# Expert loop of a gated two-layer kernel: the second product of an expert moved one place back, butterfly stages multiplied in pairs, and the shared expert spread differently over the program

## Chip, cores and metric

The kernel runs on one core of one Trainium2 chip. The metric is the device time in microseconds (us) of one execution. The engines are PE (TensorE), DVE (VectorE), ACT (ScalarE), POOL (GpSimd) and SP (SyncE, which only issues DMAs here).

## What is computed

The input is x of 4 x 1024 tokens with 256 features. Four blocks are added to it in turn, each with a gate.

```python
x = x + tanh(g_xattn[0]) * L0_xattn(layernorm(x), ctx)   # 16 heads, stablemax, 154 keys
x = x + tanh(g_ffn[0])   * L0_ffn(layernorm(x))          # 64 experts, top 8, capacity 128, + shared expert
x = x + tanh(g_xattn[1]) * L1_xattn(layernorm(x), ctx)   # softmax attention
x = x + tanh(g_ffn[1])   * L1_ffn(layernorm(x))          # butterfly MLP
```

In the L0 feed-forward block each expert works on up to 128 gathered tokens: `silu(x @ Wg) * (x @ Wu) @ Wd`, 128 inner features, scattered back with the routing weight. A shared expert with 512 inner features works on all tokens.

The L1 feed-forward block is `butterfly(gelu(butterfly(x @ W_exp + b) + up_bias)) @ W_con`. A butterfly on 1024 features has ten stages. Stage s replaces feature i by `own[i] * y[i] + other[i] * y[i ^ 2**s]`. The butterflies don't depend on x, so the kernel folds them into W_exp and W_con beforehand: after that the block is two plain products.

## The kernel before, in words

The program has three stages, with all engines drained between them. Each is a plan, a list of named units written out by `plan_first`, `plan_experts` and `plan_last`; every engine runs its own part of each unit, in the order of the plan and in no other. So a unit that waits on an engine holds up all that stands behind it on that engine.

- `plan_first`: L0 attention, over 8 halves of 512 tokens, and the gate.
- `plan_experts`: at its start 14 tiles (`TAIL_TILES` 18 to 31) of `hots` and `place`, which count tokens into the lists of the experts: DVE makes two one-hot tiles, ACT scales one, and PE adds four matmuls (L935). One step of the shared expert stands behind each tile. Then come `lists` (with a round trip through memory), three more shared steps and `tokens`. Then comes the loop over 64 experts.
- `plan_last`: L1 attention and the butterfly MLP, pipelined over the 8 halves, 20 chunks each. Half 0 has its search for the largest scores (`peak`, L987/L989 on PE, L1694 on DVE) ahead of the pipeline.

The loop takes experts in overlapping places. In iteration n the PE runs `down(n-5)` (the second product, L967), `gate_up(n-4)` (the first product, L958), `turn(n-3)` (the transposes of the gathered rows, L948), and POOL runs the scatter (L1813) of `down`'s result and the gather (L1805) of expert n. Between `gate_up(e)` and `down(e)` stand ACT's silu (L1226) and DVE's product `inner` (L1657). `gate_up(e)` itself waits for `inner(e-1)`, since both use one bank; `down(e)` waits for DVE's `made(e-1)` (L1664).

Two streams fill the gaps of the loop. `back` holds the steps of the shared expert; in one half of 512 tokens they are four steps with `sh_up` (12 matmuls of 128x512, L882), one step with none, and two `sh_down` (24 matmuls of 128x256, L898). `fusing` holds the folding of the butterflies: for seven stages of each of the two butterflies and 8 blocks of 128 features, ACT scales the identity (`stage_p`, L1182), DVE adds the scaled swap (`stage_m`, L1589), PE multiplies (`inside`, L917) and ACT brings the result back (L1189). The three other stages are `across` (ACT and DVE alone). One fusing step stands behind `down` and one behind `turn`.

`LATE = 2` says that the shared expert's last two halves (6 and 7) stand in `plan_last`, one step behind two `peak` units each; `BEHIND = 4` steps stand behind the end of the loop.

## Time and profile before

| | |
|---|---|
| median of 3 runs | 1270.5 us (1266.7 to 1273.0) |
| profiled execution | 1270.4 us, span 1268.6 us |
| busy over the span | PE 84%, DVE 63%, PEld (PE's weight load) 61%, ACT 58%, POOL 28% |
| mean granted TensorE clock | 0.919 of full speed |
| matmuls and weight loads | 5713 each; DVE 1988 instructions, ACT 1447 |
| chain that ended last | PE 52%, DVE 21%, ACT 14% |

The busy shares are means over three stages with different limits, so they don't say what one edit is worth. Ends of matmuls are modelled; the distance from one start to the next is the better measure of what a group of matmuls costs. An f32 matmul is recorded as two instructions, a rounded one (fp32r) as one.

### The profile page before, as it was taken

What the parts mean: (1) busy time and instruction counts of PE and PEld (TensorE: products, weight loads), DVE (VectorE), ACT (ScalarE), POOL (GpSimd) and SP (SyncE); (2) the same over time, 40 slices, a digit from 0 to 9 for tenths busy, and PEclk for the clock granted to TensorE, in tenths of its full rate; (3) what the DMA queues carried; (4) which work ended last, traced back from release to release, by engine and by line L of the source; (5) the groups of instructions that cost most, each with busy time, mean ns of one, the idle gap of its engine ahead of it and who ended that gap; (6) DMA issues with size and microseconds to landing.
All of it is one profiled execution on the core that took longest, in us unless ns stands there. A gap on an engine that the chain in (4) does not pass through costs nothing.

```text
span 1268.6 us, 17757 instructions
## 1 busy us (share of the span) xinstructions
PE 1063.4 (84%) x5713; PEld 770.4 (61%) x5713; DVE 802.0 (63%) x1988; ACT 732.5 (58%) x1447; POOL 357.1 (28%) x313
## 2 busy tenths in 40 slices
PE   3788888888876788998899868778989989999988
PEld 2344444444444677876688756646766767767567
DVE  4568778777777654555654476566676676765443
ACT  1998888898964335665665432344455445544542
POOL 2000000000000004777777420204253342423223
PEclk9788888898877998999999979868999999999998
DMA  6554535442120305889887352230232132220000
GB/s 152 122 134 138 141 80 156 133 113 71 51 104 33 141 18 149 210 197 226 215 208 187 52 158 65 71 98 1 77 87 86 26 102 58 64 70 1 20 17 17
DMA packets 97404, 128.44 MB, mean 101 GB/s; under 512 B 26976, under 2 KB 69344, under 8 KB 97056
## 3 DMA queue, kind: packets, MB, share of 16 engines
q1 hardware_dynamic: 83312, 106.91, 29.3%
q0 software_dynamic: 12288, 18.88, 8.2%
q10 hardware_dynamic: 1712, 1.51, 0.6%
q8 instruction: 47, 0.77, 0.3%
q14 instruction: 45, 0.37, 0.1%
HBM read 66.15 MB, written 30.70 MB: 76 GB/s over the span
## 4 chain that ended last, share of the span: by engine, by line
PE 52%; DVE 21%; ACT 14%; issue 7%; DMA 3%; SPq 2%; POOL 1%; ACTq 1%; DVEq 0%; POOLq 0%
PE psum L1055 5%; PE psum L882 5%; PE psum L1040 5%; PE psum L898 4%; PE psum L789 4%; PE psum L958 3%; PE psum L917 3%; PE psum L765 3%; ACT weights L1115 3%; PE psum L987 3%; PE psum L967 3%; ACT weights L1111 2%; PE psum L784 2%; DVE stats L1318 2%; DVE peaks L1694 2%
## 5 line engine op out<-in xcount | busy, mean ns | idle before, releaser
L1793 POOL TENSOR_SCALAR vareps<-moments 128x4 f32<-128x4 f32 x32 | 10.4, 326 | 556.9 <-DVE moments L1321 556.9
L765 PE MATMUL psum<-q_stack,k_stack 96*128 96x512 f32 (+1 forms) x256 | 128.3, 528 | 43.7 <-DVE weights L1439 20.8
L1255 ACT ACTIVATE weights<-psum 128x512 f32<-128x512 f32 x160 | 94.0, 595 | 86.9 <-PE psum L765 78.1
L1439 DVE SCALAR_TENSOR_TENSOR weights<-psum,weights 128x512 f32<-128x512 f32 x160 | 102.9, 681 | 50.7 <-ACT weights L1119 50.4
L1694 DVE TENSOR_REDUCE peaks<-psum 128x2 f32<-128x308 f32 x256 | 107.0, 468 | 16.6 <-PE psum L989 16.1
L1838 POOL TENSOR_TENSOR hidden<-hidden_whole,hidden 128x512 fp32r<-128x512 f32 x64 | 82.3, 1285 | 121.9 <-DVE hidden L1742 121.9
L1813 POOL DMA_INDIRECT expert_sums<-made,sum_rows x64 | 102.5, 1601 | 44.5 <-DVE made L1664 26.8
L987 PE MATMUL psum<-k_stack,q_stack 96*128 96x256 f32 x256 | 85.7, 382 | 34.4 <-DVE peaks L1694 24.7
L882 PE MATMUL psum<-feat_parts,w_shared_up 128*128 128x512 f32 x384 | 101.1, 415 | 7.1 <-ACT shared_silu L1166 2.8
L1111 ACT ACTIVATE weights<-psum 128x512 f32<-128x512 f32 x160 | 89.2, 598 | 24.2 <-issue 14.0
L1055 PE MATMUL psum<-w_con_high,hidden 128*128 128x256 f32 x512 | 101.8, 297 | 0.0
L1805 POOL DMA_INDIRECT got<-rows_scratch,tokens x64 | 69.0, 1079 | 115.1 <-DVE sum_rows L1651 95.9
L765 PEld LDWEIGHTS psum<-q_stack,k_stack 96*128 96x128 f32 (+1 forms) x256 | 51.3, 205 | 79.4 <-issue 34.9
L1742 DVE CAST hidden<-hidden_whole 128x512 fp32r<-128x512 f32 x64 | 49.7, 777 | 72.5 <-ACT hidden_whole L1284 71.6
L1115 ACT ACTIVATE weights<-weights 128x512 f32<-128x512 f32 x160 | 94.2, 636 | 1.0
L1119 ACT ACTIVATE weights<-weights 128x512 f32<-128x512 f32 x160 | 93.9, 633 | 1.0
L987 PEld LDWEIGHTS psum<-k_stack,q_stack 96*128 96x128 f32 x256 | 50.8, 199 | 64.4 <-DVE peaks L1694 32.4
L1040 PE MATMUL psum<-feats,w_up_high 128*128 128x512 f32 x256 | 80.7, 412 | 10.4 <-DVE feats L1734 6.6
L1055 PEld LDWEIGHTS psum<-w_con_high,hidden 128*128 128x128 f32 x512 | 80.8, 189 | 14.0 <-POOL hidden L1838 7.3
L882 PEld LDWEIGHTS psum<-feat_parts,w_shared_up 128*128 128x128 f32 x384 | 73.7, 199 | 23.4 <-ACT shared_silu L1166 3.1
L789 PE MATMUL psum<-weights,values 128*32 128x512 f32 x512 | 79.7, 699 | 2.3 <-ACT turned L1126 2.3
L1284 ACT ACTIVATE hidden_whole<-psum,hidden_bias 128x512 f32<-128x512 f32 x64 | 42.6, 687 | 62.0 <-PE psum L1040 55.6
(201 smaller groups left out, 2478.8 us busy)
## 6 DMA issues: line engine op xcount, KB each, us to landing
expert_w<-in_expert_w SPq DMA_DIRECT2D x64, 384.0 KB
q_stack<-q_stage SPq DMA_DIRECT2D x96, 128.0 KB, 2.4
q_stack<-q_stage SPq DMA_DIRECT2D x192, 64.0 KB, 2.0
expert_sums<-zeros SPq DMA_DIRECT2D x6, 1408.0 KB, 7.8
fetched<-expert_sums SPq DMA_DIRECT2D x16, 512.0 KB, 4.5
rows_scratch<-rows SPq DMA_DIRECT2D x8, 640.0 KB, 3.2
k_raw<-in_k SPq DMA_DIRECT2D x16, 300.0 KB
x<-in_x SPq DMA_DIRECT2D x8, 512.0 KB, 4.6
```

The lines of the kernel that those rows point to most:

```text
L765: T.matmul(to, k[0:row, head_at(head), :], q[0:row, head // 2, :], start=True, stop=True).then_inc(scored, 1)
L789: m = T.matmul(to[32 * j:32 * j + 32, :], vals[:, 0, 4 * g + j, :], w[(n + j) % len(w)][:, :], start=True, stop=False, tile_position=(0, 3 ...
L882: m = T.matmul(shared_banks(h).ap(key, half), w_sgu[:, pw, a:a + P], sh_parts[:, pf, c * HALF:(c + 1) * HALF], start=n == 0 and c == 0, st ...
L987: T.matmul(view[:, :, 0:P], q[0:STACK, p, t * P:(t + 1) * P], keys[0:STACK, 2 * p:2 * p + 2, :], start=True, stop=True)
L1040: m = T.matmul(wide.ap(key), up_parts[pw][:, c, k * P:(k + 1) * P], feats[:, pf, c, :], start=i == 0 and c == 0, stop=i == 2 and c == CD - 1)
L1055: m = T.matmul(out_bank[t // 2][:, t % 2 * DIM:(t % 2 + 1) * DIM], hidden[k][:, ph, t * P:(t + 1) * P], con_parts[pw][:, BURST * b + k, :] ...
L1111: A.activation(weights[n % 9][:, :], score_bank[n % 5], ACT.Relu, scale=-1.0).then_inc(clipped, 1)
L1115: A.activation(weights[n % 9][:, :], weights[n % 9][:, :], ACT.Ln, bias=1.0).then_inc(logged, 1)
L1255: A.activation(weights1[n % 6][:, :], score_bank[n % 2], ACT.Exp).then_inc(exped, 1)
L1439: V.scalar_tensor_tensor(weights[n % 9][:, :], score_bank[n % 5], 1.0, weights[n % 9][:, :], ALU.add, ALU.max).then_inc(weighted, 1)
L1694: V.tensor_reduce(peaks[h % 2][:, t, 2 * p:2 * p + 2], view, AX.X, ALU.max).then_inc(wide.frees(key, i), 1)
L1813: G.indirect_dma_start(sum_dram[e % SUMS], bass.IndirectOffsetOnAxis(ap=sum_rows[:, e:e + 1], axis=0), made[e % 4][:, :], None, bounds_che ...
```

## The change

1. `DOWN_LAG = 6`: `down(n-6)` stands where `down(n-5)` stood. The loop has 70 iterations in place of 69.
2. The seven `inside` stages are taken as four rounds: (0,1), (2,3), (4,5), (6), and in reverse for the second butterfly. A round of two stages is one matrix `own*I + a*swap + b*swap + c*both_swaps`, which DVE makes with three dependent instructions. Their 112 matmuls with `stage_m` become 64. A new unit `taps` makes the coefficients once, at the start of the loop.
3. `fusing` has 100 steps in place of 146 and is spread over the loop's first 64 iterations.
4. In the 14 tiles ahead of the loop, only every second tile has a shared step: 7 steps move into the loop.
5. `LATE = 1`: the shared expert's half 6 moves from `plan_last` into the loop, which then has 32 shared steps where it had 18. The same four kinds of step are left behind its end.
6. In `plan_last`, the sends of half 1's queries (`send_q1`, 24 DMAs on SP) stand behind the DMAs of half 0's `peaks`, not ahead of them; the first 12 sends of half h+2 stand one chunk later, which for h = 0 puts them behind the DMAs of half 1's `peaks`.

```diff
-LATE = 2
+LATE = 1
+
+DOWN_LAG = 6
...
         plan.append(("place", i))
-        back.step()
+        if i % 2:
+            back.step()
...
-    stages = (("down", 5), ("gate_up", 4), ("turn", 3), ("gather", 0))
-    share = len(back.steps) - BEHIND
-    for n in range(EXPERTS + 5):
+    stages = (("down", DOWN_LAG), ("gate_up", 4), ("turn", 3), ("gather", 0))
+    share, fuses, slot = len(back.steps) - BEHIND, len(fusing.steps), 0
+    for n in range(EXPERTS + DOWN_LAG):
...
             elif work != "gather":
-                fusing.step(1 + (n % 8 == 0 and work == "down"))
+                if slot * fuses // (2 * EXPERTS) != (slot + 1) * fuses // (2 * EXPERTS):
+                    fusing.step()
+                slot += 1
...
         if c == 12:
-            units += [("turn_q1", h + 2), ("send_q1", h + 2, 0), ("send_q1", h + 2, 1)]
+            units.append(("turn_q1", h + 2))
+        if c == 13:
+            units += [("send_q1", h + 2, 0), ("send_q1", h + 2, 1)]
...
-                    9: [("turn_q1", 1)] + [("send_q1", 1, two) for two in range(PAIRS // 2)]}
+                    9: [("turn_q1", 1)]}
...
     plan.append(("peaks", 0))
+    plan += [("send_q1", 1, two) for two in range(PAIRS // 2)]
...
+            def set_coef():
+                key, at = ("taps",), 2 * HB * len(MOVED)
+                V.wait_ge(*fused.filled(key))
+                V.tensor_copy(both_swaps[:, :, :].rearrange("p s n -> p (s n)"), fused.ap(key)[:, at:at + INSIDE // 2 * P])
+                for n, (which, i) in enumerate(MOVED):
...
             def stage_matrix(n):
...
-                V.scalar_tensor_tensor(matrix[n % 4][:, :], swaps[:, s, :], taps[:, 2 * which + 1, s, k:k + 1],
-                                       own_part[n % 2][:, :], ALU.mult, ALU.add).then_inc(matrix_set, 1)
+                m = V.scalar_tensor_tensor(to, swaps[:, stages[-1], :], coef[:, which, i, 1, k:k + 1], own_part[n % 2][:, :],
+                                           ALU.mult, ALU.add)
+                if len(stages) == 2:
+                    m.then_inc(dve_own, own.up())
+                    V.wait_ge(dve_own, own.n)
+                    V.scalar_tensor_tensor(to, swaps[:, stages[0], :], coef[:, which, i, 2, k:k + 1], to, ALU.mult,
+                                           ALU.add).then_inc(dve_own, own.up())
+                    V.wait_ge(dve_own, own.n)
+                    m = V.scalar_tensor_tensor(to, both_swaps[:, min(stages) // 2, :], coef[:, which, i, 3, k:k + 1], to,
+                                               ALU.mult, ALU.add)
+                m.then_inc(matrix_set, 1)
```

The order of PE's instructions early in the loop, before the change. The digit behind `expert_w` and `inner` is that of the buffer: L967 is `down`, L958 is `gate_up`, L948 is `turn`, L917 is `inside`.

```order
L958 MATMUL psum<-got_t1,expert_w1 128x128 x4
L948 MATMUL psum<-ident,got2 128x128 x2
L917 MATMUL psum<-butterfly_u,stage_m0 128x257
L967 MATMUL psum<-expert_w1,inner1 128x256
L917 MATMUL psum<-butterfly_u,stage_m1 128x257
L958 MATMUL psum<-got_t2,expert_w2 128x128 x4
```

The same engine and place in the changed kernel, where L987 is `gate_up`, L977 `turn`, L946 `inside`, L996 `down` and L898 `sh_up`.

```order
L987 MATMUL psum<-got_t2,expert_w2 128x128 x4
L977 MATMUL psum<-ident,got3 128x128 x2
L996 MATMUL psum<-expert_w1,inner1 128x256
L946 MATMUL psum<-butterfly_u,stage_m0 128x257
L987 MATMUL psum<-got_t0,expert_w3 128x128 x4
L898 MATMUL psum<-feat_parts,w_shared_up 128x512 x12
L977 MATMUL psum<-ident,got4 128x128 x2
```

Behind the first product of expert 1 came its own second product; now the second product of expert 1 stands behind the first product of expert 2, and there are fewer `inside` and more shared matmuls between.

DVE's instructions over about one iteration of the loop before: `made` (L1664), `stage_m`, `inner` (L1657), and a shared step (L1569, L1563).

```order
608 L1664 TENSOR_SCALAR made<-psum,got 128x256
609 L1589 SCALAR_TENSOR_TENSOR stage_m<-swaps,taps,stage_p 128x128
610 L1657 TENSOR_TENSOR inner<-silu,psum 128x128
611 L1569 TENSOR_TENSOR shared_inner<-shared_silu,shared_inner 128x512
612 L1563 TENSOR_TENSOR shared_silu<-shared_silu,psum 128x512
613 L1589 SCALAR_TENSOR_TENSOR stage_m<-swaps,taps,stage_p 128x128
```

The same place of DVE in the changed kernel.

```order
591 L1717 TENSOR_SCALAR made<-psum,got 128x256
592 L1633 SCALAR_TENSOR_TENSOR stage_m<-swaps,coef,stage_p 128x128
593 L1638 SCALAR_TENSOR_TENSOR stage_m<-swaps,coef,stage_m 128x128
594 L1641 SCALAR_TENSOR_TENSOR stage_m<-both_swaps,coef,stage_m 128x128
595 L1710 TENSOR_TENSOR inner<-silu,psum 128x128
596 L1597 TENSOR_TENSOR shared_inner<-shared_silu,shared_inner 128x512
597 L1591 TENSOR_TENSOR shared_silu<-shared_silu,psum 128x512
598 L1633 SCALAR_TENSOR_TENSOR stage_m<-swaps,coef,stage_p 128x128
```

Ahead of `inner` stand three matrix instructions, each of which reads what the one before it wrote, where one stood.

SP's DMAs at the start of the last stage before: two times 24 sends of queries (L691), the values (L1978, L1981), the peaks of half 0 (L1992), and the fetch of half 2 (L1963).

```order
87 L691 DMA q_stack<-q_stage 32x512 x24
88 L1978 DMA values_0<-in_ctx 128x16x16
89 L1981 DMA values_0<-in_ctx 26x4x16 x4
90 L691 DMA q_stack<-q_stage 32x512 x24
91 L1992 DMA q_stack<-peak_t 1x8x512 x4
92 L1963 DMA fetched<-expert_sums 128x4x256 x2
```

The same place of SP in the changed kernel.

```order
89 L707 DMA q_stack<-q_stage 32x512 x24
90 L2031 DMA values_0<-in_ctx 128x16x16
91 L2034 DMA values_0<-in_ctx 26x4x16 x4
92 L2045 DMA q_stack<-peak_t 1x8x512 x4
93 L707 DMA q_stack<-q_stage 32x512 x24
94 L2016 DMA fetched<-expert_sums 128x4x256 x2
```

The peaks' DMAs went ahead of half 1's sends; the fetch of half 2 is still behind them.

## Rows read from the trace of the kernel before

**Rows 1.** Stretches: length, busy PE, PEld, DVE, ACT, POOL, granted clock, DMA share, GB/s

```profile
421.80:471.30 49.50, 43.94 (x252) 36.91 (x253) 28.03 (x50) 18.56 (x29) 0.00 (x0) 0.93 0.25 88
483.70:497.40 13.70, 13.67 (x72) 10.62 (x73) 5.96 (x17) 8.61 (x27) 5.32 (x5) 0.88 0.31 94
497.40:703.60 206.20, 188.41 (x1125) 157.03 (x1123) 110.50 (x287) 126.68 (x373) 155.42 (x117) 0.99 0.83 203
703.60:716.30 12.70, 11.81 (x68) 9.34 (x68) 5.88 (x17) 8.56 (x27) 8.74 (x6) 1.00 0.46 68
716.30:729.80 13.50, 10.25 (x61) 9.19 (x60) 6.12 (x11) 2.18 (x3) 2.05 (x3) 0.87 0.18 21
729.80:797.20 67.40, 46.69 (x228) 39.01 (x228) 45.19 (x88) 17.66 (x27) 8.96 (x12) 0.83 0.39 108
```

**Rows 2.** PE waits of the second product in the loop, by line

```profile
L967 PE MATMUL psum<-expert_w,inner 128*128 128x256 f32 x118 | 40.2, 423 | 13.3 <-DVE inner L1657 11.1 <-issue 1.9
```

**Rows 3.** PE timeline, two iterations: start, length, what, [idle before, releaser]

```profile
539.16 3.01 PE L882 MATMUL psum<-feat_parts,w_shared_up 128*128 128x512 f32 x12
542.02 0.38 PE L948 MATMUL psum<-ident,got 128*128 128x128 f32 x2
542.23 0.60 PE L917 MATMUL psum<-butterfly_u,stage_m 128*128 128x257 f32 x2
542.67 0.59 PE L967 MATMUL psum<-expert_w,inner 128*128 128x256 f32 x2
...
543.53 1.05 PE L958 MATMUL psum<-got_t,expert_w 128*128 128x128 f32 x8
544.42 0.38 PE L948 MATMUL psum<-ident,got 128*128 128x128 f32 x2
545.41 0.70 PE L967 MATMUL psum<-expert_w,inner 128*128 128x256 f32 x2 [0.16 <-DVE inner L1657]
```

**Rows 4.** POOL timeline in the loop: one scatter, one gather, the next scatter

```profile
551.45 1.59 POOL L1813 DMA_INDIRECT expert_sums<-made,sum_rows  x1 [0.30 <-issue]
553.35 1.05 POOL L1805 DMA_INDIRECT got<-rows_scratch,tokens  x1 [0.30 <-issue]
554.71 1.59 POOL L1813 DMA_INDIRECT expert_sums<-made,sum_rows  x1 [0.31 <-issue]
```

**Rows 5.** DVE: a line's instructions (ns min/median/max), a line's busy time, a timeline

```profile
L1589 DVE SCALAR_TENSOR_TENSOR stage_m<-swaps,taps,stage_p x112: 340/350/416, 483.3 to 713.0; 128x128 f32<-128x128 f32 x112
...
L1664 DVE TENSOR_SCALAR made<-psum,got 128x256 f32<-128x256 f32 x63 | 30.4, 482 | 10.8 <-PE psum L967 8.6 <-issue 1.3 <-DMA expert_sums<-made,sum_rows 0.5
...
482.50 0.22 DVE L1644 SCALAR_TENSOR_TENSOR listed<-psum,listed 128x64 f32<-128x64 f32 x1
482.76 0.20 DVE L1647 CAST tokens<-listed 128x64 uint32<-128x64 f32 x1
```

**Rows 6.** PE timeline ahead of the loop: the second wait for a down step

```profile
453.14 4.49 PE L898 MATMUL psum<-w_shared_down,shared_inner 128*128 128x256 f32 x24 [2.35 <-DVE shared_inner L1569]
```

**Rows 7.** Timelines of DVE, SP, PE, POOL at the start of the last stage

```profile
784.37 1.62 DVE L1694 TENSOR_REDUCE peaks<-psum 128x2 f32<-128x308 f32 x4
819.59 1.39 DVE L1318 BATCH_NORM_STATS2 stats<-x 128x6 f32<-128x256 f32 x4
...
777.44 15.40 SPq L691 DMA_DIRECT2D q_stack<-q_stage  x24
792.89 2.72 SPq L1992 DMA_DIRECT2D q_stack<-peak_t  x4
...
831.32 7.56 SPq L691 DMA_DIRECT2D q_stack<-q_stage  x12
...
797.83 4.43 PE L898 MATMUL psum<-w_shared_down,shared_inner 128*128 128x256 f32 x24
843.28 0.80 PE L765 MATMUL psum<-q_stack,k_stack 100*128 100x512 f32 x1 [4.56 <-DMA q_stack<-peak_t]
...
799.70 4.92 POOL L1828 TENSOR_TENSOR x<-x,fetched 128x1024 f32<-128x1024 f32 x2 [30.56 <-DMA fetched<-expert_sums]
```

70 lines of the change are left out of this document (48 added, 22 removed).

## Prediction

> **What bounds the kernel now.** I read the busy shares by stretch first, then the timelines of PE, DVE, POOL and SP at the edges that the change touches, then the waits in the loop. Three stretches matter [rows 1]: the 14 tiles ahead of the loop (421.8 to 471.3, PE busy 43.9 of 49.5 us), the loop (483.7 to 716.3) and the start of the last stage (729.8 to 797.2, with PE and DVE both well under full). In the loop PE is busy 188 of 206 us, but POOL is busy 155 of the same 206 and stands idle for 0.3 us ahead of each issue: scatter to scatter takes 554.71 - 551.45 = 3.26 us when it waits for nobody [rows 4]. So two engines are near their limits there, PE at about 3.5 us an iteration and POOL with a floor of 3.26. The reader should see that moving work into the loop is not free, and that the loop can't shrink by much either.
>
> **Prices, from starts to starts [rows 3].** A loaded shared step 542.02 - 539.16 = 2.86, taken as 2.8 us (a down step is alike); turn 0.21; inside 0.44; gate_up 544.42 - 543.53 = 0.89; down 0.43 (543.53 - 542.67 = 0.86 for one down and one inside). From the end of a first product (544.42) to its second product (545.41) pass 0.99 us when nothing else is in the way: silu, `inner`, semaphores. Between them PE has only turn and one inside (0.65), so it waits some 0.3 us in each iteration without a shared step. One listing puts 13.3 us of such waits on the second product [rows 2], not counting the refill of the pipeline behind each.
>
> **Term 1, the tiles ahead of the loop: -21.** Seven of 14 shared steps leave: four up steps, two down steps and one without matmuls. Six loaded steps x 2.8 = 16.8. With them goes the second of two waits for the last shared product: 2.35 us of idle, after which the 24 matmuls took 4.49 us in place of 2.8, some 1.6 more [rows 6]; the granted clock of the stretch is 0.93, so PE ran at 1.2 GHz for a part of it and at 2.4 for the rest [rows 1]. Sum 20.8. The tiles that stay bare must not become a bound of their own: of PE's 43.9 busy us 33.6 are the twelve loaded steps, so the 14 tiles cost it 6 to 10, and it needs 23 to 27 us after; of DVE's 28.0 the moved steps (four products and four differences of a 128x512 tile, two additions of a half's rows) hold 7 to 8, which leaves it 20. So PE stays the longer one. Bounds: -16.8 (waits not saved) to -22. What stands between this stretch and the loop (the lists, three shared steps, the tokens) is made of the same steps as before and keeps its length.
>
> **Term 2, the loop's first 64 iterations: +2.** PE's work before: 60 gate_up (53.4), 61 turn (12.8), 59 down (25.4), 102 inside (44.9), four turns of the folded matrix (3.5) and 16 loaded shared steps (44.8): 184.8 us, in 703.6 - 483.7 = 219.9. So 35 us are waits of all kinds. After: 53.4 + 12.8 + 24.9 + 64 inside (28.2) + 3.5 + 28 loaded shared steps (78.4) + the new `taps` products (1.3, from 0.22 for each of three 128x128 products and 0.1 for six small ones) = 202.5 us. The waits: (a) in an iteration without a shared step the second product no longer waits, since a whole iteration lies between; the next gate_up waits for `inner` instead, but has turn, down and mostly an inside ahead of it (1.08 against 0.99). Only 36 such iterations are left where 48 were. (b) At the start DVE must make the coefficients (15 small instructions, at 0.26 from start to start [rows 5] some 4 us, beside a down step on PE) and its first matrices cost three times as much. Up to the first scatter PE has the `taps` (1.3), three shared steps (8.4), seven insides (3.1), two gate_up, three turns and a down (2.8): 15.6, with 2.4 of waits 18, where 13.7 were [rows 1]. (c) The across steps still stand in DVE's way as before. I take 19 us of waits: 221.5, or +1.6.
>
> DVE's part: a matrix instruction takes 0.35 [rows 5], and a dependent one starts 0.04 after the end of its predecessor (482.50 + 0.22 = 482.72 against 482.76 [rows 5]). So a paired matrix costs 0.35 x 3 + 0.04 x 2 + 0.04 = 1.17. There are 48, and 16 single ones: 62 us in place of 39. With two more halves' worth of shared work (14 to 16 us) DVE goes from 116 busy of 220 to about 155. In an iteration without a shared step DVE has `made` 0.48 [rows 5], `inner` some 0.3 and 1.17 to 2.34 of matrices against PE's 2.0 to 2.4: the two nearly touch. Behind a late matrix stand `inner`, and for it gate_up; I put 0.1 us per iteration into the 19 for that. Bounds of the waits: 6 us (PE at the pace of POOL, 58 x 3.26 = 189 from first scatter to last gather) and 35 (as many as before).
>
> At POOL, one place of the Trainium skill speaks against this. First the row: a scatter takes 1.59 and a gather 1.05 with 0.30 between, while matrix builds run on DVE beside them [rows 4]. The Trainium skill, "SBUF — State Buffer", section "SBUF: two separate sides", says that VectorE and GpSimd share a port pair as an exclusive lock, which a VectorE operation with two SBUF inputs also takes against a GpSimd operation that reads SBUF. The 48 additional matrix instructions are of that kind. By the page POOL could be held 48 x 0.35 = 17 us longer; by the row, where such instructions already run beside it, nothing is to be seen, and I put nothing into the sum.
>
> **Term 3, the loop's tail: -4.** Before, the five last iterations take 12.7 us with ten fusing steps in them [rows 1]. After, they hold none: four times 0.89 + 0.99 + 0.05 and then two second products, 0.43 + 0.48 for what `made` holds back: 8.5 us. POOL ends its six scatters of 1.9 us at about the same time, so the last one is hidden behind the four shared steps that still follow, which keep their 13.5 us [rows 1]. Bounds: -5 to 0.
>
> The moved loads (512 KB a half, on SP's queue behind the expert weights) have six iterations of lead. An expert's weights are now asked for one iteration later, since SP waits for `down`; they still come four iterations early.
>
> **Term 4, the start of the last stage: -9.5.** Four loaded steps leave the search for peaks, where two units cost DVE 1.62 [rows 7] and each shared step 2.8 more on PE in a chain with DVE: 4 x 2.4 = 9.6, I take 9. Without edit 6 this would be lost, since SP issues the 24 sends until 777.44 + 15.40 = 792.84 and the peaks at 792.89. Two down steps leave as well (4.43 for the first and some 3 for the second [rows 7]): 16 in all. Then it is given back in part. Half 1's first peaks need the first six sends, which now start behind the peaks' DMAs: 3.4 us of waiting on PE with all scores behind it, 13 left. The fetch of half 2 stands behind all 24 sends, 15.4 later against the peaks' DMAs: POOL's additions start at 799.70 - 9 + 15.4 = 806.1 and end 4.92 later, at 811.0. DVE wants its statistics at 819.59 - 13 = 806.6 and waits 4.4; behind it stand the remaining peaks of half 1. 8.6 left. Then half 1's scores: the wait of 4.56 at 843.28 for the peaks' DMAs [rows 7], which stood behind 12 sends of 7.56 us, goes; in its place PE waits some 3.3 us for half 2's first six sends, now behind the peaks. 1 more: 9.6. Bounds: -3 (only what SP's reordering can't lose) to -18 (no given-back waits, and full clock).
>
> **Sum.** 1270.4 (the profiled execution's own time; span 1268.6; the median is 1270.5) - 21 + 1.6 - 4 - 9.6 = 1237.4, rounded to 1237. Nothing before 421.8 or in halves 2 to 7 of the last stage changes.
>
> **Rivals.**
> - *The loop keeps its waits.* DVE's three-step matrices make `inner` late, so that as much is lost as before: 35 us in place of 19, +16: 1253. For it: DVE nearly touches PE in iterations without a shared step. Against it: DVE was idle in half the stretch. 0.18.
> - *POOL becomes the bound*, by the lock or by denser transfers (DMA share 0.83 already [rows 1]): a cycle of 3.8 in place of 3.26 gives 58 x 3.8 = 220 against PE's 203, +17: 1254. Against it: the row shows no lengthening. 0.05.
> - *The loop runs at POOL's floor* and the clock holds: waits fall to 6, -13: 1224. 0.09.
> - *Slower than before.* Each paired matrix stands wholly in the path of its inside product and of the `inner` behind it: 48 x (1.17 - 0.35 + a wait of 0.1) = 44 us, with the 7 + 7 moved steps not absorbed: 1237 + 44 = 1281. It decides from 34/48 = 0.7 us a matrix on. Against it: matrices are made two steps ahead. 0.05.
> - *No change to be measured*: the loop takes back all of term 1 and half of term 4, between 1264 and 1277. 0.05.
>
> **How the numbers follow.** The forecast has 0.58, its own range 1228 to 1247. The range must leave out no more than 0.2: 1222 to 1256 takes in the floor case and the first two rivals. A measurement of this kernel tells 0.5%, 6.4 us, from no change: faster 0.90, same 0.05, slower 0.05.
>
> **What would show it.** Right: the stretch ahead of the loop near 28 us; from the tokens to the last second product 228 to 232 us; second products that wait for nothing and gate_up with short waits for `inner`; 24 sends issued behind the peaks' DMAs, and DVE waiting for the additions of half 2. Wrong: a loop over 240 us, POOL cycles over 3.4 us without a wait, matrix builds over 1.3 us, or a last stage that is no shorter.

## The result

| | before | changed |
|---|---|---|
| median | 1270.4 us (4 runs) | 1256.7 us (4 runs: 1251.2, 1254.1, 1259.3, 1260.1) |
| ratio | | 0.9885, 95% interval 0.985 to 0.992 |
| profiled execution, span | 1268.6 us | 1258.3 us |
| mean granted clock | 0.919 | 0.906 |

The change makes the kernel 13.7 us faster. Of all runs in this document two (one of a2_tiles, one of d1_all) fell in a slower state of the chip; the ratios leave them out, the medians do not. The forecast was 1237 us, with a range of 1222 to 1256: the gain is less than half of it, and the time is 0.7 us outside the range.

**Stretches of the kernel after**, with the columns of [rows 1]: the tiles, the lists, from the tokens to the first scatter, from there to the last second product, the drain behind it, and the start of the last stage up to the first scores.

```profile
421.80:452.80 31.00, 28.47 (x162) 23.86 (x163) 20.30 (x40) 14.45 (x22) 0.00 (x0) 0.89 0.34 123
452.80:464.40 11.60, 6.50 (x29) 5.63 (x27) 6.41 (x15) 1.63 (x3) 0.00 (x0) 0.71 0.49 142
464.20:489.60 25.40, 21.63 (x119) 18.37 (x120) 15.49 (x55) 10.13 (x29) 6.35 (x7) 0.93 0.28 93
489.60:711.20 221.60, 201.94 (x1256) 171.19 (x1255) 139.80 (x360) 116.01 (x321) 162.08 (x119) 1.00 0.80 192
711.20:723.80 12.60, 9.14 (x62) 8.05 (x60) 5.43 (x9) 2.17 (x3) 4.89 (x4) 1.00 0.37 42
723.80:783.10 59.30, 39.08 (x180) 33.04 (x180) 39.34 (x79) 12.00 (x18) 8.86 (x12) 0.71 0.32 88
```

Against before: the tokens come at 464.2 in place of 483.2, 19 us earlier. From the tokens to the last second product it takes 247.0 us in place of 232.7, so 14 of the 19 are given back. The drain is 1.3 us shorter, the start of the last stage 8 (67.5 to 59.3), and the rest of the last stage 4 us longer.

**The waits of PE in the loop**, by line, 489.6 to 711.2 (line, operands, count | busy us, mean ns | idle us before, and who ended it). [Rows 2] had 13.3 us on the second product; now 6.6 stand there and 10.6 on the first product.

```profile
L987 PE MATMUL psum<-got_t,expert_w 128*128 128x128 f32 x488 | 67.0, 280 | 10.6 <-DVE inner L1710 5.8 <-ACT got_t L1247 3.1 <-issue 0.6
...
L996 PE MATMUL psum<-expert_w,inner 128*128 128x256 f32 x124 | 38.0, 388 | 6.6 <-DVE made L1717 3.8 <-issue 1.6 <-DVE inner L1710 0.9
```

**One iteration without a shared step and one with it, on PE**, as a timeline:

```profile
671.86 1.05 PE L987 MATMUL psum<-got_t,expert_w 128*128 128x128 f32 x8
672.75 0.38 PE L977 MATMUL psum<-ident,got 128*128 128x128 f32 x2
672.97 0.60 PE L946 MATMUL psum<-w_con_fused,stage_m 128*128 128x256 f32 x2
673.40 0.59 PE L996 MATMUL psum<-expert_w,inner 128*128 128x256 f32 x2
674.49 1.13 PE L987 MATMUL psum<-got_t,expert_w 128*128 128x128 f32 x8 [0.50 <-DVE inner L1710]
675.38 3.12 PE L914 MATMUL psum<-w_shared_down,shared_inner 128*128 128x256 f32 x24
678.34 0.38 PE L977 MATMUL psum<-ident,got 128*128 128x128 f32 x2
678.56 0.60 PE L946 MATMUL psum<-w_con_fused,stage_m 128*128 128x256 f32 x2
678.99 0.59 PE L996 MATMUL psum<-expert_w,inner 128*128 128x256 f32 x2
679.42 0.59 PE L946 MATMUL psum<-w_con_fused,stage_m 128*128 128x256 f32 x2
679.85 1.05 PE L987 MATMUL psum<-got_t,expert_w 128*128 128x128 f32 x8
```

**The same time on DVE:**

```profile
672.64 0.48 DVE L1717 TENSOR_SCALAR made<-psum,got 128x256 f32<-128x256 f32 x1
673.03 0.34 DVE L1633 SCALAR_TENSOR_TENSOR stage_m<-swaps,coef,stage_p 128x128 f32<-128x128 f32 x1
673.41 0.35 DVE L1638 SCALAR_TENSOR_TENSOR stage_m<-swaps,coef,stage_m 128x128 f32<-128x128 f32 x1
673.80 0.35 DVE L1641 SCALAR_TENSOR_TENSOR stage_m<-both_swaps,coef,stage_m 128x128 f32<-128x128 f32 x1
674.07 0.28 DVE L1710 TENSOR_TENSOR inner<-silu,psum 128x128 f32<-128x128 f32 x1
```

The first product ends at 672.75 (where the next products start), ACT's silu starts at 673.01, and `inner` could follow at 673.3. It starts at 674.07, since a matrix of three instructions stands ahead of it. So from a first product's end to the next one's start 1.74 us pass, where I had counted 0.99. In the next iteration PE is busy for 3 us with a shared step: it waits for nobody, and the other engines wait for it. The two iterations take 679.85 - 671.86 = 7.99 us, with one idle time of 0.50 on PE. POOL has more:

**POOL over four iterations** (scatter starts and what each waited for; compare [rows 4], 3.26 from scatter to scatter):

```profile
669.29 1.59 POOL L1866 DMA_INDIRECT expert_sums<-made,sum_rows  x1 [0.31 <-issue]
...
673.93 1.69 POOL L1866 DMA_INDIRECT expert_sums<-made,sum_rows  x1 [1.68 <-DVE made L1717]
...
677.28 1.59 POOL L1866 DMA_INDIRECT expert_sums<-made,sum_rows  x1 [0.31 <-issue]
...
681.92 1.69 POOL L1866 DMA_INDIRECT expert_sums<-made,sum_rows  x1 [1.70 <-DVE made L1717]
```

Scatters are 4.64, 3.35 and 4.64 apart: 8.0 us for two iterations. In the one POOL idles for `made`, in the other it runs at its floor. The pair shown is among the longer ones: of the 63 distances from scatter to scatter 37 are at most 3.4 us, 13 lie up to 4.2 and 13 above. Short and long alternate in most of the loop.

### The profile page after: what moved, and what is told of

The parts are those of the page before. It is cut to its first block, busy times and chain, and to the rows that moved or that the text cites. A ratio compares the mean times of both kernels' runs of the same rounds, so it can differ in the third digit from the quotient of the medians.

```text
span 1258.3 us, 17472 instructions
## 1 busy us (share of the span) xinstructions
PE 1052.7 (84%) x5635; PEld 764.0 (61%) x5635; DVE 821.2 (65%) x2051; ACT 702.6 (56%) x1351; POOL 358.4 (28%) x313
## 4 chain that ended last, share of the span: by engine, by line
PE 48%; DVE 24%; ACT 12%; issue 7%; DMA 4%; POOL 1%; SPq 1%; ACTq 1%; POOLq 0%; DVEq 0%
PE psum L1084 5%; PE psum L1069 5%; PE psum L898 5%; PE psum L805 4%; PE psum L987 3%; PE psum L914 3%; PE psum L781 3%; PE psum L1016 3%; DVE peaks L1747 2%; ACT weights L1144 2%; DVE stats L1346 2%; DMA expert_sums<-made,sum_rows 2%; DVE normed L1387 2%; DVE weights L1467 2%; ACT weights L1140 2%
## 5 line engine op out<-in xcount | busy, mean ns | idle before, releaser
L781 PE MATMUL psum<-q_stack,k_stack 96*128 96x512 f32 (+1 forms) x256 | 131.2, 538 | 41.3 <-DVE weights L1467 22.8
L1016 PE MATMUL psum<-k_stack,q_stack 96*128 96x256 f32 x256 | 94.7, 421 | 35.0 <-DVE peaks L1747 19.8
L1866 POOL DMA_INDIRECT expert_sums<-made,sum_rows x64 | 103.9, 1624 | 60.0 <-DVE made L1717 35.7
L898 PE MATMUL psum<-feat_parts,w_shared_up 128*128 128x512 f32 x384 | 100.5, 413 | 8.7 <-DVE shared_silu L1591 4.0
L1140 ACT ACTIVATE weights<-psum 128x512 f32<-128x512 f32 x160 | 88.9, 597 | 23.1 <-issue 13.7
L1016 PEld LDWEIGHTS psum<-k_stack,q_stack 96*128 96x128 f32 x256 | 57.3, 224 | 67.4 <-DVE peaks L1747 26.6
L1069 PE MATMUL psum<-feats,w_up_high 128*128 128x512 f32 x256 | 80.1, 410 | 10.9 <-DVE feats L1787 7.1
L898 PEld LDWEIGHTS psum<-feat_parts,w_shared_up 128*128 128x128 f32 x384 | 73.2, 197 | 24.9 <-DVE shared_silu L1591 4.4
L987 PE MATMUL psum<-got_t,expert_w 128*128 128x128 f32 x512 | 70.3, 280 | 11.3 <-DVE inner L1710 6.4
```

Of the source, the lines that this page charges most:

```text
L781: T.matmul(to, k[0:row, head_at(head), :], q[0:row, head // 2, :], start=True, stop=True).then_inc(scored, 1)
L898: m = T.matmul(shared_banks(h).ap(key, half), w_sgu[:, pw, a:a + P], sh_parts[:, pf, c * HALF:(c + 1) * HALF], start=n == 0 and c == 0, st ...
L987: m = T.matmul(bank[2][:, part * P:(part + 1) * P], expert_w[e % 8][:, c, part * INNER:(part + 1) * INNER], got_t[e % 3][:, c, :], start=c ...
L1016: T.matmul(view[:, :, 0:P], q[0:STACK, p, t * P:(t + 1) * P], keys[0:STACK, 2 * p:2 * p + 2, :], start=True, stop=True)
L1069: m = T.matmul(wide.ap(key), up_parts[pw][:, c, k * P:(k + 1) * P], feats[:, pf, c, :], start=i == 0 and c == 0, stop=i == 2 and c == CD - 1)
L1140: A.activation(weights[n % 9][:, :], score_bank[n % 5], ACT.Relu, scale=-1.0).then_inc(clipped, 1)
```

## The experiments

All eighteen were timed beside the kernel before, whose median was 1269.7 to 1271.6 us each time. The profiles can be compared by stretch, which is sharper than the medians: the first stage, which no kernel here changes, ends anywhere from 418 to 429 us and moves all that follows. The tokens count as there where DVE starts the last list, `sum_rows`. The table holds the length of each stretch in each profiled execution: from the second stage's first load to the tokens ("tiles"), to the first scatter ("start"), to the last second product ("loop"), to the last stage's first fetch ("drain"), to the first scores ("search"), to the end ("rest").

| kernel | median | ratio to before, interval | tiles | start | loop | drain | search | rest |
|---|---|---|---|---|---|---|---|---|
| before | 1270.4 | | 60.6 | 14.2 | 218.5 | 13.9 | 67.5 | 471.4 |
| changed | 1256.7 | 0.9885 (0.985 to 0.992) | 42.1 | 25.4 | 221.6 | 12.6 | 59.3 | 475.2 |
| a1_lag5 | 1270.2 | 1.0003 (0.9975 to 1.0032) | 41.3 | 18.5 | 245.5 | 13.8 | 59.9 | 475.1 |
| a2_tiles | 1261.5 | 0.9914 (0.9881 to 0.9948) | 60.9 | 25.4 | 208.9 | 13.9 | 59.4 | 475.1 |
| a3_single | 1256.3 | 0.989 (0.9839 to 0.9941) | 41.4 | 21.2 | 231.8 | 13.8 | 57.5 | 464.3 |
| a4_late2 | 1248.7 | 0.983 (0.9795 to 0.9864) | 42.2 | 25.3 | 210.6 | 12.6 | 66.8 | 471.8 |
| b1_sends | 1262.9 | 0.9941 (0.9919 to 0.9964) | 42.4 | 26.0 | 221.6 | 12.4 | 67.1 | 467.3 |
| b2_taps | 1252.8 | 0.9855 (0.9827 to 0.9882) | 43.7 | 22.3 | 223.1 | 12.4 | 57.7 | 471.0 |
| b3_dummy | 1253.2 | 0.9861 (0.9832 to 0.9889) | 42.4 | 25.4 | 225.3 | 12.7 | 60.1 | 470.5 |
| b4_downs | 1250.3 | 0.9851 (0.9813 to 0.989) | 42.2 | 25.3 | 221.7 | 12.4 | 54.2 | 470.0 |
| c1_halves | 1238.3 | 0.977 (0.9725 to 0.9814) | 41.8 | 20.5 | 210.3 | 13.8 | 59.9 | 462.4 |
| c2_onestep | 1248.4 | 0.9817 (0.9785 to 0.985) | 41.3 | 23.6 | 216.3 | 13.9 | 59.8 | 475.1 |
| c3_distance | 1266.8 | 0.998 (0.996 to 1.0) | 60.5 | 16.1 | 214.1 | 13.9 | 66.8 | 471.0 |
| c4_pairs | 1272.4 | 1.0011 (0.9992 to 1.003) | 60.6 | 21.0 | 215.0 | 13.8 | 68.1 | 471.7 |
| d1_all | 1233.8 | 0.97 (0.9658 to 0.9742) | 45.3 | 18.5 | 212.6 | 13.9 | 53.8 | 460.8 |
| d2_all_late2 | 1238.0 | 0.973 (0.9701 to 0.976) | 43.0 | 18.4 | 205.0 | 14.1 | 64.6 | 471.1 |
| d3_halves_single | 1251.2 | 0.9839 (0.9807 to 0.9872) | 39.5 | 20.7 | 225.9 | 12.3 | 57.7 | 473.7 |
| d4_halves_lag5 | 1234.7 | 0.9735 (0.9693 to 0.9777) | 41.8 | 16.1 | 220.6 | 12.4 | 59.0 | 462.1 |
| e1_best_lag5 | 1242.8 | 0.9762 (0.9716 to 0.9807) | 45.3 | 15.2 | 220.4 | 13.9 | 54.1 | 470.3 |
| e2_warm | 1236.0 | 0.9725 (0.9697 to 0.9753) | 45.2 | 18.6 | 214.0 | 12.4 | 58.1 | 464.2 |

Where two kernels share the code of a stretch ahead of the last stage, it agrees within 4 us (tiles 41.3 to 42.4, loop 221.6 to 225.3), so a smaller difference of one stretch says little by itself. The interval of the changed kernel overlaps or touches those of a2, a3, a4, b1, b2, b3, b4, c2 and d3: there the reading rests on the stretches. The column "rest" differs by more than that with the same code, and gets a part of its own below.

### The parts, undone one at a time

**a1_lag5**: the second product one place behind the first.

```diff
-DOWN_LAG = 6
+DOWN_LAG = 5
```

> The changed kernel with the second product one place behind the first again (lag 5). Theory A (the distance gives what I priced: some 0.3 us in each of the 30 to 40 iterations without a shared step, some 1 us at the seven matrices that are late): 8 to 12 us slower than the changed kernel, with 13 us or more of waits in front of the second product in place of 6.7. Theory B (in the loop's stretch the wait only moves from the second product to the first, which waits for inner 6.4 us and for got_t 3.1 in the changed kernel, and the scatter's distance sets the pace): within 3 us of the changed kernel; the first products' waits of 11.3 us shrink by what the second products' grow.

Theory A, and more than it said: 13.5 us by the medians, 17 in start and loop together. The second product now waits 28.2 us in the loop:

```profile
482.80:728.30 245.50, 213.03 (x1286) 181.14 (x1286) 145.04 (x369) 119.90 (x332) 165.25 (x122) 0.98 0.74 176
...
L996 PE MATMUL psum<-expert_w,inner 128*128 128x256 f32 x126 | 42.2, 418 | 28.2 <-DVE inner L1710 28.2
```

**a2_tiles**: a shared step after every tile again.

```diff
-        if i % 2:
-            back.step()
+        back.step()
```

> The changed kernel with a shared step after each of the 14 tiles again, as in the kernel before (7 steps leave the loop). The sum in the prediction had 16.8 to 20.8 us saved ahead of the loop against 6 x 2.8 = 16.8 us more work in the loop, of which most would stand in waits. Theory A (each moved step costs the loop nearly its full 2.8 us, since PE had no waits to give: the loop grew by 14 us): the tokens come 19 us later and the loop is 15 to 19 us shorter, total within 4 us of the changed kernel. Theory B (the loop grew for the matrices and its start instead): the loop is only 5 to 10 us shorter and the total 9 to 14 us slower.

Between the theories: the tiles are 18.8 us longer, the loop 12.7 shorter. So part 4 of the change is worth 4.8 us by the medians (their intervals overlap), 6.1 by tiles and loop, and each of the seven steps costs the loop 1.8 us.

**a3_single**: no pairs, one matrix a stage, and the fusing steps placed as in the kernel before; the rest as changed (the kernel before with parts 1, 4, 5 and 6). It undoes parts 2 and 3 together; no run parts them.

```diff
-LATE = 2
+LATE = 1
...
-        back.step()
+        if i % 2:
+            back.step()
...
-    stages = (("down", 5), ("gate_up", 4), ("turn", 3), ("gather", 0))
+    stages = (("down", 6), ("gate_up", 4), ("turn", 3), ("gather", 0))
```

> The changed kernel without the pairing: one matrix a stage (112 inside products, one vector instruction each), no taps, and the fusing steps placed as in the kernel before; distance, tiles, last stage and sends as changed. PE has 48 inside products more (48 x 0.44 = 21 us) and 1.3 us of taps less, DVE 23 us less, ACT 48 x 0.8 = 38 us more. Theory A (pairing frees PE, and PE bounds the loop): 12 to 20 us slower than the changed kernel. Theory B (the three-step matrices and the coefficients at the start take back what PE saves): within 5 us, with the first scatter 5 to 8 us after the tokens earlier than the 25.4 us of the changed kernel, and the steady part of the loop 5 to 10 us longer.

Neither in full. Pairs save 10.2 us of loop and cost 4.2 of start; PE's busy time in the loop falls by 16 us (218.0 to 201.9), so a third of what PE saves turns into waits. Start and loop together are 6.0 us shorter with pairs. The equal medians don't show it: "rest" is 10.9 us shorter in a3_single's profile than in the changed kernel's, with the same text, and the two intervals reach 4 and 7 us to each side.

**a4_late2**: the shared expert's half 6 back in the last stage.

```diff
-LATE = 1
+LATE = 2
```

> The changed kernel with the shared expert of the two last halves beside the search for peaks again (7 steps leave the loop, the sends stay where the change puts them). Theory A (the last stage was shortened by 9 us by my sum, the loop grew by 16.8 for these seven steps less the waits they fill): with the last stage 538 to 540 us against 534.4 and the loop 10 to 15 us shorter than 247: 6 to 10 us faster than the changed kernel. Theory B (steps in the loop are half hidden in waits): loop 6 to 8 us shorter, last stage 5 us longer: within 3 us. If the granted clock of the stretch 40 to 80 us behind the start of the last stage is again 0.8 or more (changed kernel 0.50 in 35 us, before 0.85), the missing 5 us of the last stage are the clock's.

Theory A: 8 us faster than the changed kernel, and the clock is up as well (0.90 in the first 20 us of scores, "rest" 3.4 us shorter). The seven steps cost the loop 11.0 us and save 7.5 in the search. Part 5 is a loss here: 3.5 us by these two stretches, what is over of the 8 goes with "rest".

**b1_sends**: the sends of half 1 and (not shown) those of half h+2 where they were.

```diff
-    plan.append(("peaks", 0))
-    plan += [("send_q1", 1, two) for two in range(PAIRS // 2)]
+    plan.append(("peaks", 0))
...
-                    9: [("turn_q1", 1)]}
+                    9: [("turn_q1", 1)] + [("send_q1", 1, two) for two in range(PAIRS // 2)]}
```

> The changed kernel with the sends of half 1 and half 2 where the kernel before has them (ahead of the DMAs of half 0's peaks, and at chunk 12). Theory A (as in the prediction: SP would issue the peaks' DMAs only behind 24 sends of 15.4 us, so that the 9 us saved ahead of the peaks are lost, while the wait of 2.4 us for half 1's first sends goes and half 2's rows come earlier): the first product of scores some 8 to 10 us later than in the changed kernel, total 4 to 8 us slower. Theory B (the order of the sends only moves waits): within 3 us.

Theory A: 6.2 us slower, search 67.1 in place of 59.3. In the profiles "rest" goes the other way by 7.9 us, at granted clocks of 0.68 and 0.83 in its first two stretches of 20 us where the changed kernel has 0.50 and 0.55. So the 7.8 us hold for the search, and the 6.2 for the whole kernel rest on the medians. Part 6 is what lets four steps less among the peaks be worth anything, as the prediction had it.

### The start and the last stage

**b2_taps**: taps and coefficients after tile 26 (not shown: the first inside product waits for the tokens in the taps' place, and the tokens' product for the coefficients).

```diff
-            steps += [[("taps",)], []] + inside
+            steps += inside
...
+        if i == TILES - 6:
+            plan.append(("taps",))
...
```

> The changed kernel with the taps products and the coefficients made ahead of the loop, after tile 26 of 32, in place of the first fusing steps behind the tokens; the first inside product waits for the tokens in their place. Theory A (the first scatter comes 25.4 us after the tokens in place of the 18 that I counted because taps, coefficients and the first matrices stand in a row, each waiting for the last): first scatter 4 to 6 us earlier, total 3 to 6 us faster. Theory B (POOL and PE make up for a late start later in the loop, since neither is full all the time): first scatter earlier by as much, the last second product at the same time within 1.5 us, total the same within 3 us.

Start 3.1 us shorter, tiles 1.6 and loop 1.5 longer: by these stretches the gain is swallowed, as Theory B has it. The median is 3.9 us less, as Theory A has it, but the intervals overlap, and in the profile it is search (1.6) and "rest" (4.2) that are shorter. **The start of the changed kernel on PE** shows what stood in a row there; the last two lines are of DVE:

```profile
464.59 1.48 PE L925 MATMUL psum<-taps,swaps 128*128 128x16 f32 x12 [1.99 <-DVE sum_rows L1704]
465.92 1.58 PE L929 MATMUL psum<-swaps 128*128 128x128 f32 x6
467.15 4.10 PE L914 MATMUL psum<-w_shared_down,shared_inner 128*128 128x256 f32 x24
473.26 0.70 PE L946 MATMUL psum<-butterfly_u,stage_m 128*128 128x257 f32 x2 [2.00 <-DVE stage_m L1641]
474.30 0.70 PE L946 MATMUL psum<-butterfly_u,stage_m 128*128 128x257 f32 x2 [0.34 <-DVE stage_m L1641]
475.33 0.70 PE L946 MATMUL psum<-butterfly_u,stage_m 128*128 128x257 f32 x2 [0.34 <-DVE stage_m L1641]
...
471.30 0.87 DVE L1605 SCALAR_TENSOR_TENSOR x<-psum,sgate,x 128x256 f32<-128x256 f32 x2 [1.95 <-PE psum L914]
472.09 0.34 DVE L1633 SCALAR_TENSOR_TENSOR stage_m<-swaps,coef,stage_p 128x128 f32<-128x128 f32 x1
```

The taps take 2.56 us (counted: 1.3), the down step 4.1 at a granted clock of 0.73 (2.8), the first matrix is waited for 2.0, and the next inside products follow at DVE's pace, 1.03 apart in place of 0.44. The coefficients were not what the first matrix waited for: they were done at 469.35, but in DVE's order the addition of the down step stands ahead of it, and DVE waited 1.95 us for that step's products.

**b4_downs**: the two last shared down steps behind half 0's peaks, in PE's wait for their DMAs.

```diff
-LATE_AT = (1, 3, 5, 7, 9, 11, 13)
+LATE_AT = (1,)
...
-    late.step()
+    late.step(2)
     plan.append(("scores1", 0))
```

> The changed kernel with the two shared down steps of the last half moved from among the peaks to behind half 0's last peaks, into PE's wait of 5.7 us for the peaks' DMAs. They are 5.5 and 3.1 us long where they stand. Theory A (they lengthen the search for peaks where they are, and are hidden in the wait): the first product of scores 4 to 6 us earlier, unless the 48 products take longer than the DMAs (at half clock some 9 to 10 us against 6.7: then 1 to 3 us earlier), and the clock high from there: total 4 to 8 us faster. Theory B (DVE's peaks, 0.94 us a unit, and the sends bound the search): within 2 us of the changed kernel, since in place of PE's products DVE's waits grow.

Theory A: 6.4 us faster by the medians, search 54.2 in place of 59.3. The search tells it, since the intervals overlap.

**b3_dummy**: seven idle products in that wait.

```diff
+                if n == 0:
+                    T.wait_ge(*late.freed(("sh_down", HALVES - 1, HT // 2 - 1)))
+                    for _ in range(7):
+                        T.matmul(bank[3], q1_stack[0][0:STACK, 0, 0:P], k1_stack[0][0:STACK, 0:4, :], start=True, stop=True)
```

> The changed kernel with seven products of 128x512 that nobody reads, on PE in the wait of 5.7 us ahead of the first scores of the last stage (into a bank that is free there). It adds work and no use. Theory A (the last stage lost about 5 us to the granted clock, which is 0.50 from 46 to 81 us behind the stage's start, where it was 0.85 before): the clock rises within or right behind these products, the scores, peaks and weighted sums behind them run at 2.4 GHz, and the kernel is 3 to 6 us faster in spite of the added work. Theory B (PE's clock there costs nothing, since DVE's peaks and DMAs set the pace): same within 2 us, whatever the clock does.

The median is 3.5 us lower, but no more than that can be said: "rest" is 470.5, and in b2_taps, without any such products, it is 471.0. See below on the clock.

### The loop

**c1_halves**: each shared step of the tiles and the loop cut in two; one half behind each tile, six ahead of the tokens, eight behind the loop. A `part` runs one half of the products on PE.

```diff
+def halved(steps):
+    out = []
+    for step in steps:
+        first = [u for u in step if u[0] not in ("sh_up", "sh_down")]
+        second = []
+        for u in step:
+            if u[0] in ("sh_up", "sh_down"):
+                first.append(("part", u, 0))
+                second += [("part", u, 1), u]
+        out += [first, second]
+    return out
...
-        back.add(("shared", h), shared_steps(h)[0 if h else SHARED_EARLY:])
+        back.add(("shared", h), halved(shared_steps(h)[0 if h else SHARED_EARLY:]))
...
```

> The changed kernel with each shared step of the tiles' and the loop's stretches cut in two halves of six or twelve products (half of the vector and scalar work follows with the second), one half after each tile and, in the loop, after nearly each first product. Same work, same order, other grain. Theory A (POOL bounds the short iterations at its floor of 3.26 us and PE bounds those with a whole shared step at some 4.4, so that the loop runs at the mean of the longer of the two, (28 x 4.4 + 36 x 3.3) / 64 = 3.8 us, and not at the longer of the two means): with iterations all alike PE needs some 3.4, the stretch from first scatter to last second product falls from 221.6 to 205 to 212 us, total 8 to 15 us faster. Theory B (the loop grew for latencies in a row, matrices, inner, semaphores, that stay as they are): within 4 us.

Theory A for the loop: 210.3 us. The total falls by 18.4 us where the theory had 8 to 15. By the stretches ahead of "rest" 14.7 us of it are the halves' (start 4.9, loop 11.3 and tiles 0.3 less, drain and search 1.8 more); what is over goes with a "rest" that is 12.8 us shorter in the profile, with the same text. **Its loop as one stretch, then by line:**

```profile
483.70:693.90 210.20, 198.10 (x1256) 170.94 (x1255) 139.89 (x360) 115.99 (x322) 162.52 (x120) 1.00 0.84 202
...
L1003 PE MATMUL psum<-got_t,expert_w 128*128 128x128 f32 x488 | 66.6, 279 | 6.9 <-ACT got_t L1263 4.5 <-DVE inner L1726 0.8
...
L1012 PE MATMUL psum<-expert_w,inner 128*128 128x256 f32 x126 | 38.1, 384 | 3.7 <-DVE made L1733 3.4
...
L1882 POOL DMA_INDIRECT expert_sums<-made,sum_rows x62 | 100.6, 1623 | 41.4 <-DVE made L1733 20.4 <-issue 19.8 <-DMA expert_sums<-made,sum_rows 1.2
```

The work is the same (POOL 162.6 us busy in the loop, 162.1 in the changed kernel; DVE 140.0 and 139.8). What went is waiting: the first product's for `inner` from 5.8 to 0.8 us, POOL's for `made` from 35.7 to 20.4 (of which 16.3 and 11.4 are the wait of the very first scatter, so 19.4 to 9.0 in the loop). The loop's number was right, but the trace doesn't bear out the cause that Theory A gave, POOL's floor in the short iterations: in these two loops the profile puts no wait of PE down to a gather or a scatter. What it shows is that half a shared step now stands in nearly every iteration and covers the 1.74 us from first product to first product.

**c2_onestep**: two of a paired matrix's three vector instructions left out (the folded weights lack two of four terms).

```diff
-                if len(stages) == 2:
+                if False:
```

> The changed kernel with the second and third vector instruction of each paired matrix left out (the product's other two terms are missing from the folded weights; PE, ACT and POOL do the same work). It takes 96 instructions of 0.35 us, 34 us with 0.04 between, from DVE. Theory A (DVE's three-step matrices are what keeps the pairing from paying, as inner and made stand behind them): the loop is 8 to 15 us shorter, first scatter 2 to 3 us earlier. Theory B (DVE was half idle and the pace is set by PE and POOL): loop within 3 us, only the start 1 to 2 us shorter. If POOL and DVE shared a lock that these instructions hold, scatters and gathers would also shorten by up to 34 us in sum; their busy sum in the loop of 173 us would fall.

Between the two: loop 5.3 and start 1.8 us shorter. The two further instructions of the paired matrices cost that much, and not the 16 us of start and loop that halving the steps gives. POOL is busy for 161.1 us in this loop and for 162.1 in the changed kernel's, so taking away 96 vector instructions with two SBUF inputs (34 us of them) freed POOL of some 1 us.

**c3_distance** and **c4_pairs**: the kernel before with one part each.

```diff
-    stages = (("down", 5), ("gate_up", 4), ("turn", 3), ("gather", 0))
+    stages = (("down", 6), ("gate_up", 4), ("turn", 3), ("gather", 0))
...
-    for n in range(EXPERTS + 5):
+    for n in range(EXPERTS + 6):
```

c4_pairs is the changed kernel with `DOWN_LAG = 5`, `LATE = 2`, a step behind each tile and the sends as before: parts 2 and 3 alone.

> The kernel before with the second product two places behind the first and nothing else. Undoing this alone in the changed kernel cost 13.5 us (median), 17 in the loop. Theory A (the distance saves the waits of 13.3 us on the second product in any mix of work): 6 to 13 us faster than before. Theory B (it pays only with many shared steps in the loop, since it lets gathers and scatters bridge long iterations; in the kernel before, with 20 steps among 64 iterations, PE has other work): within 4 us of before.

> The kernel before with the stages folded by pairs (taps, coefficients, three-step matrices, fusing steps spread over the slots) and nothing else. PE has 48 inside products less (21 us), ACT 96 instructions less, DVE 23 us more. Undoing it alone in the changed kernel left the time the same (1256.3 against 1256.7), with 6 us more in the loop. Theory A (PE bounds the loop before): 10 to 18 us faster than before. Theory B (POOL's floor and the waits take it up: the kernel before already runs at 3.4 us an iteration, 3.26 is the floor): at most 5 us faster, with the first scatter 4 to 7 us later and the rest of the loop 8 to 12 us shorter.

Theory B in both totals. The distance alone gives 2.9 us (interval 0.996 to 1.0) where it gives 13.5 inside the change; pairs alone give nothing (2.7 us more than before, interval 0.999 to 1.003). In c4_pairs the first scatter comes 6.8 us later, as expected, but the rest of the loop is only 3.5 us shorter and not 8 to 12. **The loop of before and of c4_pairs, then the second product of each:**

```profile
497.40:715.90 218.50, 199.82 (x1190) 165.99 (x1188) 116.38 (x303) 135.01 (x399) 163.76 (x122) 0.99 0.81 195
...
L967 PE MATMUL psum<-expert_w,inner 128*128 128x256 f32 x125 | 42.7, 423 | 14.2 <-DVE inner L1657 11.8 <-issue 2.1
```

```profile
507.70:722.70 215.00, 182.19 (x1106) 151.31 (x1105) 129.22 (x344) 109.27 (x315) 164.76 (x122) 0.99 0.83 198
...
L992 PE MATMUL psum<-expert_w,inner 128*128 128x256 f32 x126 | 42.1, 416 | 23.6 <-DVE inner L1706 23.6
```

PE is busy 17.6 us less. The wait for `inner` grows by 11.8.

**d3_halves_single** (a3_single with halved steps, so without parts 2 and 3) and **d4_halves_lag5** (c1_halves with `DOWN_LAG = 5`):

> The single stages (112 inside products, one vector instruction each) with the shared steps in halves; distance, tiles, last stage and sends as changed. PE has 21 us more inside products than with pairs. Theory A (with even iterations PE bounds the loop, so pairing pays in full): loop of 222 to 230 us in place of 210, start 1 to 4 us shorter, total 8 to 17 us slower than the same kernel with pairs (1238). Theory B (PE and POOL share the bound and the three-step matrices cost as much as they save): within 4 us of 1238.

> The kernel with halved shared steps and the second product one place behind the first. Theory A (the distance was needed since a whole shared step and a late matrix hold up inner and made; with halves the second product has turn, inside and 1.4 us of shared products between, more than the 0.99 that the way from first to second product takes): 0 to 4 us slower than 1238. Theory B (the distance bridges PE's in-order waits for the matrices, whatever the grain): 10 to 17 us slower, as with whole steps.

Theory A in the first, but for the start, which is no shorter. With halves, pairing is worth 12.8 us (1251.2 against 1238.3; loop 225.9 against 210.3): PE is busy 216 of 226 us in d3_halves_single and is the bound. In the second neither theory in full: by the medians the distance is worth nothing (1234.7 against 1238.3, intervals overlapping). By the stretches some 4.5 us are left of it: the loop is 10.3 us longer without it, the start 4.4 and the drain 1.4 shorter, and the second product waits 10.5 us for `inner` in place of 28.2 in a1_lag5.

### Versions that are faster

**d1_all** is c1_halves with b2_taps and b4_downs; **d2_all_late2** has half 6 in the last stage besides; **e1_best_lag5** is d1_all with `DOWN_LAG = 5`.

> The kernel with halved shared steps, with the taps and coefficients after tile 26 and the two last shared down steps behind half 0's last peaks: the three edits that were faster than the changed kernel by 18, 4 and 6 us. If they add up: 1228 to 1232 us. If the early taps are swallowed by the loop, as the edit makes only its start shorter and the rest ends at POOL's pace: 1231 to 1235. Stretches: first scatter 16 to 18 us after the tokens (20.5 with halves alone), loop 210, search 54 to 55 (59.9).

> As d1_all, with the shared expert of the two last halves in the last stage (14 steps there: four ahead of the peaks, six among them, two behind them, two among the first scores). With whole steps in the loop this gave 8 us over the changed kernel. Theory A (with halves the loop is at POOL's floor, 58 x 3.26 = 189 and more, and PE's 3.4 us an iteration are only just above it, so that the loop gains at most 0.15 us x 58 = 9 us from seven steps less, and the last stage loses 9 to 11): 0 to 4 us slower than d1_all. Theory B (each step in the loop still costs 1.6 us as with whole steps, 11 for seven, and the last stage grows by 7.5 and keeps a higher clock): 3 to 7 us faster than d1_all.

> d1_all (halved shared steps, early taps, down steps behind the peaks; 1234 us) with the second product one place behind the first. Theory A (with halves the distance only moves waits; with whole steps it was worth 13.5 us): within 4 us of d1_all; the start up to the first scatter 3 to 5 us shorter (one iteration less ahead of it), the stretch from there to the last second product longer by 5 to 10, drain 1 to 2 shorter. Theory B (distance matters once coefficients are early): 5 us or more slower.

d1_all takes 1233.8 us, 0.970 of before: 23 us faster than the changed kernel. The three edits don't add up: against c1_halves the search is 6.1 us shorter, but the start's 2.0 are lost again in tiles (3.5) and loop (2.3), as in b2_taps. d2_all_late2 is 4.2 us slower than d1_all, close to its Theory A. With even iterations half 6 no longer costs more in the loop (7.6 us) than it saves in the search (10.8). e1_best_lag5 is 9 us slower by the medians, but its interval and that of d1_all overlap, and in the profiles 9.5 us stand in "rest"; start, loop and drain together are 4.5 us longer, as between d4_halves_lag5 and c1_halves. So with halves the distance is worth some 4.5 us by the stretches, and within 0 to 9 by the medians.

**e2_warm**: an idle product of 128x512 ahead of each of half 0's peak units 4 to 15 in d1_all.

```diff
+                if h == 0 and HT * two + t >= 4:
...
+                    T.matmul(bank[3], q[0:STACK, 0, 0:P], keys[0:STACK, 0:4, :], start=True, stop=True)
```

> d1_all with one product of 128x512 that nobody reads ahead of each of half 0's peak units 4 to 15 (12 products, 0.40 us each at 2.4 GHz and 0.8 at 1.2). It adds work and no use. Theory A (PE's half idle search, DVE bound at 0.94 us a unit, lets the granted clock fall, and up to 13 us are lost to it in the 70 us behind; d1_all's own runs lie between 1224.8 at a mean clock of 0.92 and 1244.8 at 0.898): the median falls to 1225 to 1229 and the spread of the runs shrinks. Theory B (the clock of the later 70 us is set by other things than this stretch): same median within 3 us or slower by 2 to 5 us, since at half clock the products stretch the search.

Theory B: the search is 4.3 us longer, the median 2.2 us higher. The runs lie closer together (1231.8 to 1240.1, where d1_all has 1224.8 to 1242.1), but the lowest are gone and not only the highest.

## Why the prediction was wrong, point by point

**Term 1, tiles, -21: right, -19.** The tokens come 19.0 us earlier (60.6 to 42.1 is 18.5). In the sixteen profiles with this edit the stretch is 39.5 to 45.3 long, in the four without it 60.5 to 60.9.

**Term 2, the loop's first 64 iterations, +1.6: wrong; this is the step that failed.** From the tokens to the first product of the last iteration but four (702.32) pass 238.1 us. The prediction had 202.5 of work and 19 of waits, 221.5. Take off the same work, and 35.6 us of waits are left: as many as before (35), where the sum took them down to 19. So the term that failed is the 16 us of waits that the sum gave up. That is the first rival ("the loop keeps its waits", +16, 1253, chance 0.18), and its price was right to 1 us. Its mechanism is only a part. In place of the second product's wait for `inner` came the first product's, and the start was longer: by the distances from start to start, 14.1 us over the prices stand behind the second products (7.5 before), where the first product waits, and 15.3 behind turn and inside (25.2 before). The sum took three things wrongly:
- *The start*, counted at 18 us, took 25.4: the taps, a shared down step that DVE's first matrix stands behind, a matrix of three instructions and the first inside products follow each other in a row, at a granted clock of 0.93 over the stretch. b2_taps, c2_onestep and c1_halves each take 2 to 5 us off it.
- *Waits for `inner` at the first product*, counted at 0.1 us an iteration: 0.66 in the short iteration shown above (1.09 from the second product to the next first one in place of 0.43). That one is among the worst: the loop has 16 such waits that the profile sees, 5.8 us in sum. DVE's three-step matrix stands ahead of `inner`. c2_onestep prices the two further instructions of each at 7 us for start and loop (28.2 us of waits are left there by the count above).
- *The mean.* The sum added up PE's work over 64 iterations. But with whole shared steps in nearly every second iteration, long and short ones alternate. A short one holds 0.89 + 0.21 + 0.44 + 0.43 = 1.97 us of PE's work, and from its first product to the next one pass 0.89 + 1.74 = 2.63 in the one shown, through `silu`, the matrix and `inner`. PE can't fill this gap with the shared products of the next iteration, since they stand behind the product that waits. c1_halves shows it: same work, other grain, 16 us less in start and loop. Counted as above, from the tokens (463.09) to the same product (685.00), it takes 221.9 us, 19.4 of them waits: what the prediction had for the changed kernel (221.5 and 19).

POOL's floor, to which the prediction compared PE's work, is not what held PE up: in the changed kernel's loop the profile puts no wait of PE down to a gather or a scatter, and DVE's `made` waited for a scatter once, 0.4 us. Nor were all of the 35 us idle time that could be filled: the profile has PE idle for 17.8 us of the stretch before and for 22.0 after. In the remainder the starts lie farther apart than the prices say while the profile counts PE as busy; a clock below 1.0 and waits that the modelled ends hide would both do that, and no run here parts them.

That also tells where the single parts' gains went. Each of a tile's seven steps was to cost the loop its 2.8 us of PE work less waits filled, and cost 1.8; the seven of half 6 cost 11.0 for 7.5 saved. Pairing saves 16 to 18 us of PE. With whole steps it cost 3.3 us of start and loop in the kernel before (c4_pairs) and gave 6.0 inside the change (a3_single); with halves it gives 15.8, and 12.8 by the medians (d3_halves_single).

**Term 3, the tail, -4: right.** From 702.32 to the last second product 8.9 us, counted 8.5. The drain, which the sum left as it was, became 1.3 us shorter (13.9 to 12.6).

**Term 4, the last stage, -9.6: half of it.** The first scores come 8.2 us earlier in the stage, as counted (-9). **The order on SP** is as predicted (compare [rows 7]):

```profile
778.80 2.74 SPq L2045 DMA_DIRECT2D q_stack<-peak_t  x4
781.58 15.37 SPq L707 DMA_DIRECT2D q_stack<-q_stage  x24
797.00 1.16 SPq L2016 DMA_DIRECT2D fetched<-expert_sums  x2
```

Half 1's first peaks waited for the sends, counted 3.4:

```profile
786.73 0.58 PE L1016 MATMUL psum<-k_stack,q_stack 96*128 96x256 f32 x1 [2.37 <-DMA q_stack<-q_stage]
...
798.10 0.91 DVE L1747 TENSOR_REDUCE peaks<-psum 128x2 f32<-128x308 f32 x2 [2.08 <-PE psum L1018]
...
801.16 4.85 POOL L1881 TENSOR_TENSOR x<-x,fetched 128x1024 f32<-128x1024 f32 x2 [37.05 <-DMA fetched<-expert_sums]
```

What had no place in the sum: DVE waits for PE's peaks there (2.54 and 2.08 us), since PE runs at a granted clock of 0.50, 1.2 GHz (0.56 us a product of 256 columns, 0.36 at 2.4). The half's statistics start at 810.46, 4.4 us behind the end of POOL's additions (806.01): they were late for the peaks, and the wait of 4.4 us for POOL did not come. What the clock took is told below.

**Sum.** With the same edges in both kernels (the tokens, 703.6 or 702.32, and the start of the last second product) -21 became -19, +1.6 became +17.7 (238.1 against 220.4), -4 became -3.4 and 1.3 less for the drain, -9.6 became -4.4: 1270.4 - 19 + 17.7 - 3.4 - 1.3 - 4.4 = 1260.0 against 1260.1 measured. The median of the changed kernel is 3.4 us below its profiled run, which had one of its lower clocks.

**POOL and VectorE's port.** The prediction put nothing for the shared port of the Trainium skill ("SBUF — State Buffer", section "SBUF: two separate sides"), which by its estimate could have held POOL for up to 17 us. c2_onestep decides: without the 96 instructions POOL's busy time is 1 us less. The sign "POOL cycles over 3.4 us without a wait" came in five of 63 cycles (3.43 to 4.14 us, with a gather of up to 1.94 or a scatter of up to 1.84 in them; two before, 3.41 and 3.42): 2.1 us over the floor in all, too little to bound the loop. The sign "a loop over 240 us" came (247.0), "matrix builds over 1.3 us" did not (1.12 in the one shown). The tiles are 31.0 us long, where "near 28" was a sign of being right, and second products still wait for 6.6 us.

## What the runs showed of the hardware

The text from the search for peaks on is the same in nine of the kernels (the changed one, a1, a2, a3, b2, c1, c2, d3, d4), yet "rest" takes from 462.1 to 475.2 us in their profiles. It goes with the granted clock of its first 70 us. **The changed kernel** in stretches of 20, 20 and 30 us from the first scores, then **c1_halves**:

```profile
783.10:803.00 19.90, 17.49 (x60) 12.68 (x60) 8.02 (x17) 5.86 (x10) 1.84 (x1) 0.50 0.52 145
803.00:823.00 20.00, 16.18 (x65) 11.79 (x64) 15.93 (x39) 6.62 (x12) 6.11 (x10) 0.55 0.23 54
823.00:853.00 30.00, 23.77 (x83) 13.79 (x83) 19.87 (x38) 12.70 (x22) 6.22 (x5) 0.64 0.33 90
```

```profile
767.70:787.70 20.00, 17.20 (x71) 11.82 (x75) 9.43 (x23) 6.52 (x12) 2.02 (x1) 0.63 0.51 145
787.70:807.70 20.00, 13.93 (x69) 9.01 (x61) 16.23 (x37) 10.20 (x18) 5.94 (x10) 0.83 0.25 57
807.70:837.70 30.00, 23.38 (x123) 15.52 (x124) 21.15 (x46) 14.26 (x23) 10.87 (x7) 0.94 0.32 88
```

At 0.50, 0.55 and 0.64 the rest takes 475.1 or 475.2 us (changed, a1, a2, c2); at 0.59, 0.66 and 0.62 it takes 473.7 (d3); at 0.67, 0.83 and 0.56 it takes 471.0 (b2); at 0.63 to 0.66, 0.83 and 0.83 to 0.94 it takes 462.1 to 464.3 (a3, c1, d4). So some 13 us go with a clock that the same instructions get in one kernel and not in another. The runs' times go the same way: d1_all has one of 1224.8 us at a mean clock of 0.919 and one of 1242.1 at 0.902. The Trainium skill, "TensorE: Matmul & The Clock Gate", section "Part 1: The HAM clock gate (the "warmup" mystery)", says of the ramp to the full rate that the same kernel shows another number of products at the lower rate from run to run, and puts the ramp penalty below 1% of a typical span. The loss here is another one than the ramp's, in the middle of the kernel: 13 us, 1.0% of this span; no run here measures the ramp's.

Filling PE's waits with idle products did not buy the clock back in time (b3_dummy unclear, e2_warm 2 us slower). What decides it here stays open; that the clock causes the difference in time, and not the other way round, is argued from PE's products of 0.56 in place of 0.36 us and not shown by an experiment that sets the clock alone.

## What to carry to other kernels

- When an in-order engine is near its bound, compare its work in each single iteration with the way through the other engines that the next iteration waits for, and not by sums. Cutting the filler into equal pieces, one for each iteration, was worth as much here (18 us, 15 of them by the stretches) as all six parts of the change together (14).
- Work that is taken from an engine is time only where that engine is what the next step waits for. Here 17.6 us less PE work took 3.5 off the loop in one schedule, and with even iterations 17.9 us less took off 15.6.
- What a new unit at the head of a loop costs is its chain of instructions, with what stands ahead of them in each engine's order, and not its sum. And where a stage's rest goes with the clock, compare kernels by stretches: two medians were equal here where start and loop differed by 6 us.
